# Gated cross-attention and mixture-of-experts block: the second expert product with the high and low part of its weights side by side

## The reference, cut to what matters

```python
x = x + tanh(g_xattn[0]) * xattn(layernorm(x), ctx_768, Wq, Wk, Wv, Wo, bo)
# feed-forward: top 2 of 8 experts, capacity cap = 2 * (4096 / 8) = 1024
de = disp.reshape(E, cap, Dm)                                  # 8 x 1024 x 256
h = relu(einsum('ecd,ehd->ech', de, fc1_w) + fc1_b)            # hidden width 1024
eo = einsum('ech,ehd->ecd', h, fc2_w) + fc2_b                  # back to width 256
out = sum(gathered * (gates * w)[:, :, None], axis=1)
x = x + tanh(g_ffn[0]) * out
```

## Time and profile before

| | |
|---|---|
| median of 3 runs | 991.46 us (989.94 to 992.4) |
| the profiled execution | 994.87 us |
| its span, first to last instruction | 993.1 us |
| mean granted TensorE clock | 0.983 |
| TensorE matmul / weight load busy | 949.4 us (96%) / 823.4 us (83%) |
| VectorE, ScalarE, GpSimd busy | 676.3 us (68%), 508.1 us (51%), 281.8 us (28%) |

### The profile page before, as it was taken

The page is one execution under the profiler, slowest core; times in us unless marked ns, Lnnn a source line. Parts: engine busy times, 40 slices in busy tenths (PEclk is TensorE's granted clock), DMA queues, the critical chain, the costliest instruction groups (busy, mean ns, idle before and its releaser), DMA issues.

```text
span 993.1 us, 18998 instructions
## 1 busy us (share of the span) xinstructions
PE 949.4 (96%) x7199; PEld 823.4 (83%) x7199; DVE 676.3 (68%) x1542; ACT 508.1 (51%) x1573; POOL 281.8 (28%) x293
## 2 busy tenths in 40 slices
PE   7799999999999999999999888999999999999996
PEld 5587877888878878878888786999999999999995
DVE  5768687686785886886776862757575665657572
ACT  3567376465664773673754621535444343435352
POOL 6803025024033043042041133222222223232222
PEclk8989999999999999999999998999999999999998
DMA  9096003011020021021011015254342435252521
GB/s 259 22 298 194 22 2 107 23 41 67 22 86 24 22 92 38 2 86 44 1 44 44 13 52 187 66 117 101 76 128 50 128 49 130 49 130 56 141 53 22
DMA packets 63099, 76.63 MB, mean 77 GB/s; under 512 B 6033, under 2 KB 55096, under 8 KB 63008
## 3 DMA queue, kind: packets, MB, share of 16 engines
q1 hardware_dynamic: 50720, 59.18, 20.0%
q0 software_dynamic: 12288, 16.23, 9.0%
HBM read 46.52 MB, written 29.49 MB: 77 GB/s over the span
## 4 chain that ended last, share of the span: by engine, by line
PE 73%; ACT 11%; DVE 8%; POOL 3%; DMA 2%; issue 2%; SPq 1%; POOLq 0%; DVEq 0%; another core or an unknown queue 0%
PE down L1211 6%; PE down L1210 6%; PE down L1209 6%; PE up L1195 6%; PE up L1196 6%; PE up L1197 6%; PE score L545 4%; ACT probs_odd L733 4%; ACT work L733 4%; PE out_bank L533 4%; PE probT L520 4%; DVE negmax L913 2%; PE rT L1179 2%; PE query_bank L466 2%; PE query_bank L464 2%
## 5 line engine op out<-in xcount | busy, mean ns | idle before, releaser
L1151 POOL DMA_INDIRECT out_dram<-eo,index x64 | 99.4, 1553 | 282.2 <-ACT eo L1253 250.4
L1245 ACT ACTIVATE hid<-up,b 128x512 f32<-128x512 f32 x128 | 88.3, 690 | 84.8 <-PE up L1197 84.8
L733 ACT ACTIVATE probs_odd<-score,negmax 128x128 f32<-128x128 f32 x256 | 91.3, 382 | 44.6 <-DVE negmax L913 44.6
L733 ACT ACTIVATE work<-score,negmax 128x128 f32<-128x128 f32 x256 | 91.4, 383 | 42.8 <-DVE negmax L913 42.8
L407 POOL DMA_INDIRECT disp<-packed,slots x64 | 68.8, 1075 | 133.8 <-DVE slots L904 92.4
L913 DVE TENSOR_REDUCE negmax<-score 128x4 f32<-128x512 f32 x128 | 82.0, 682 | 28.1 <-PE score L545 27.7
L698 ACT ACTIVATE k_sb<-key_bank 128x512 f32<-128x512 f32 x64 | 38.8, 606 | 112.8 <-PE key_bank L489 111.5
L1253 ACT ACTIVATE eo<-eo_raw,gate 128x256 f32<-128x256 f32 x64 | 30.9, 506 | 122.4 <-DVE eo_raw L1315 122.4
L1306 DVE TENSOR_TENSOR hid_l<-hid,hid_h 128x512 fp32r<-128x512 f32 x128 | 88.6, 693 | 4.4
L921 DVE COPY pT<-probT 128x512 f32<-128x512 f32 x128 | 82.2, 682 | 8.7 <-PE probT L520 7.4
L1315 DVE TENSOR_TENSOR eo_raw<-down,b 128x256 f32<-128x256 f32 x64 | 25.8, 423 | 86.4 <-PE down L1211 86.4
(11 more groups left out here) (253 smaller groups left out, 2788.8 us busy)
## 6 DMA issues: line engine op xcount, KB each, us to landing
rows<-disp SPq DMA_DIRECT2D x18, 516.0 KB, 5.4
w_raw<-fc1T_dram SPq DMA_DIRECT2D x9, 1024.0 KB, 8.3
w_raw<-fc_dram SPq DMA_DIRECT2D x9, 1024.0 KB, 10.9
disp<-fixed SPq DMA_DIRECT2D x1, 8256.0 KB, 33.8
rows<-x_dram SPq DMA_DIRECT2D x16, 512.0 KB, 4.3
out_dram<-rows SPq DMA_DIRECT2D x8, 512.0 KB, 3.1
c_raw<-ctxT_dram SPq DMA_DIRECT2D x8, 256.0 KB
c_raw<-ctxT_dram SPq DMA_DIRECT2D x16, 128.0 KB
```

The costliest lines, as they stand in the source:

```text
L733: last = nc.scalar.activation(probs[w % 2][:, c, :], score[hh][:, b * P:(b + 1) * P], ACT.Exp, bias=negmax[:, w % 2, c:c + 1], accum_out=s ...
L1151: pool.indirect_dma_start(out=out_rows[:, :], out_offset=bass.IndirectOffsetOnAxis(ap=index[half][:, i:i + 1], axis=0), in_=eo[half][:, i, ...
L1245: nc.scalar.activation(hid[m % 2][:, :], up[m % 2][:, :], ACT.Relu, bias=b1[par][:, m:m + 1]).then_inc(s_hid, 1)
```

## The change

The two halves of the split second weights become one tensor, with high and low part of the same `k` next to each other. One matmul of 512 columns multiplies `hid_h` with both; its result for the low part lands in the upper 256 columns of the bank. The product `hid_l` x high part stays a matmul of 256 columns and adds into the lower half. For the last `k` the small matmul goes first, so that the wide one is the last of its block. VectorE then adds the bias to the upper half into a new tile `small_part`, waits for that instruction by a semaphore, and adds the lower half. `wo_h` and `wo_l` of the attention become views of the new tensor. ScalarE and VectorE write the weight parts through the same views, with the same element counts.

```diff
-        w2_split = [... sbuf_tensor(f"w2_split{n}", [P, HK, D], mybir.dt.float32r)) for n in range(2)]
+        w2_both = keep.enter_context(nc.sbuf_tensor("w2_both", [P, HK, 2, D], mybir.dt.float32r))
...
-    (wq_h, wq_l), (wo_h, wo_l) = w1_split, w2_split
+    wq_h, wq_l = w1_split
+    wo_h, wo_l = w2_both[:, :, 0, :], w2_both[:, :, 1, :]
...
-    w2_h, w2_l = [w2_split[0], sb("w2_h1", [P, HK, D], f32r)], [w2_split[1], sb("w2_l1", [P, HK, D], f32r)]
+    w2 = [w2_both, sb("w2_both1", [P, HK, 2, D], f32r)]
...
+    small_part = sb("small_part", [P, GB, D])
...
                 t = slice(i * P, (i + 1) * P)
-                o = down[i][:, 0:D]
-                mm(o, hid_h[:, k, t], w2_h[par][:, k, :], start=(k == 0), stop=False)
-                mm(o, hid_h[:, k, t], w2_l[par][:, k, :], start=False, stop=False)
-                last = mm(o, hid_l[:, k, t], w2_h[par][:, k, :], start=False, stop=(k == HK - 1))
+                if k == HK - 1:
+                    mm(down[i][:, 0:D], hid_l[:, k, t], w2[par][:, k, 0, :], start=False, stop=False)
+                last = mm(down[i][:, :], hid_h[:, k, t], w2[par][:, k, :, :].rearrange("p s d -> p (s d)"), start=(k == 0),
+                          stop=(k == HK - 1))
+                if k < HK - 1:
+                    mm(down[i][:, 0:D], hid_l[:, k, t], w2[par][:, k, 0, :], start=False, stop=False)
                 if k == HK - 1:
                     last.then_inc(s_down_ready, 1)
...
-            nc.scalar.activation(w2_h[par][:, :, :], w2_raw[:, :, :], ACT.Copy).then_inc(s_w_hi, 1)
+            nc.scalar.activation(w2[par][:, :, 0, :], w2_raw[:, :, :], ACT.Copy).then_inc(s_w_hi, 1)
...
-            V.tensor_tensor(w2_l[par][:, :, :], w2_raw[:, :, :], w2_h[par][:, :, :].bitcast(f32),
+            V.tensor_tensor(w2[par][:, :, 1, :], w2_raw[:, :, :], w2[par][:, :, 0, :].bitcast(f32),
                             ALU.subtract).then_inc(s_w_lo, 1)
...
-                V.tensor_tensor(eo_raw[:, i, :], down[i][:, 0:D], b2[par][:, :], ALU.add).then_inc(s_eo_raw, 1)
+                V.tensor_tensor(small_part[:, i, :], down[i][:, D:2 * D], b2[par][:, :], ALU.add).then_inc(s_small_part, 1)
+                dve.wait_ge(s_small_part, 4 * n + i + 1)
+                V.tensor_tensor(eo_raw[:, i, :], down[i][:, 0:D], small_part[:, i, :], ALU.add).then_inc(s_eo_raw, 1)
```

More of the change, by code:

```diff
@@ L96, in gated_block @@
         w1_split = [keep.enter_context(nc.sbuf_tensor(f"w1_split{n}", [P, DK, H], mybir.dt.float32r)) for n in range(2)]
-        w2_split = [keep.enter_context(nc.sbuf_tensor(f"w2_split{n}", [P, HK, D], mybir.dt.float32r)) for n in range(2)]
+        w2_both = keep.enter_context(nc.sbuf_tensor("w2_both", [P, HK, 2, D], mybir.dt.float32r))
         s_e0_lo = sem("e0_lo")
-        shared = (s_e0_lo, first, blank, running, tanh_g, ident, w1_raw, w2_raw, w1_split, w2_split)
+        shared = (s_e0_lo, first, blank, running, tanh_g, ident, w1_raw, w2_raw, w1_split, w2_both)
         block = keep.enter_context(nc.Block())
@@ L126, in sb @@
         return ctx.enter_context(nc.sbuf_tensor(name, shape, dt))
-    s_e0_lo, first, blank, running, tanh_g, ident, w1_raw, w2_raw, w1_split, w2_split = shared
-    (wq_h, wq_l), (wo_h, wo_l) = w1_split, w2_split
+    s_e0_lo, first, blank, running, tanh_g, ident, w1_raw, w2_raw, w1_split, w2_both = shared
+    wq_h, wq_l = w1_split
+    wo_h, wo_l = w2_both[:, :, 0, :], w2_both[:, :, 1, :]
     wk_h, wk_l, wk_d = (sb(n, [P, INNER], f32r) for n in ("wk_h", "wk_l", "wk_d"))
@@ L1084, in experts @@
         s_rt_ready, s_rt_hi, s_rt_split, s_up_ready, s_hid, s_hid_hi, s_hid_split, s_down_ready, s_eo_raw,
-        s_eo_raw2, s_eo_ready, s_scatter0, s_scatter1, s_meta, s_dve_self, s_pool_gate,
+        s_eo_raw2, s_small_part, s_eo_ready, s_scatter0, s_scatter1, s_meta, s_dve_self, s_pool_gate,
     ) = (sem("e_" + name) for name in (
@@ L1088, in experts @@
         "rt_ready", "rt_hi", "rt_split", "up_ready", "hid", "hid_hi", "hid_split", "down_ready", "eo_raw",
-        "eo_raw2", "eo_ready", "scatter0", "scatter1", "meta", "dve_self", "pool_gate",
+        "eo_raw2", "small_part", "eo_ready", "scatter0", "scatter1", "meta", "dve_self", "pool_gate",
     ))
```

## The result

The changed kernel takes 991.99 us (median of 22 runs, 990.25 to 993.6), the kernel before 990.09 us (22 runs, 988.43 to 992.4). The ratio is 1.0018, 95% interval 1.0011 to 1.0025: **slower by 0.18% or 1.8 us** (the medians differ by 1.9), with little doubt about the sign, where 3.5 us less was forecast. The forecast of 987.9 us counted from 991.46 for the kernel before, which took 1.4 less this time; so the change is further off the forecast (5.4) than the time itself (4.1).

The account below looks back on a forecast made before the run. TensorE's own gapless stream was taken as the bound in the expert part. 11 long down products saving 0.35 us each (3.84) less 0.29 lost at the end gave -3.55: 991.46 - 3.55 = 987.9 us, range 985.0 to 992.0.

Parts of the forecast that it names:

- A set in the long products: Down products of 11.39 us: the matmuls per `k` and block fall from 353.1 to 342.2 ns, saving 0.35 us a product.
- The short products: The 4 of 16 down products at 10.98 us: matmuls per `k` and block stay at 340.0 ns, no gain.
- It is not the place of the data: Down products: the extra 4.4 ns per narrow matmul is not from data place; groups 3 and 4 read the same weights.
- The second addition: VectorE, each block: sums come 0.46 us later, costing 0 at the 15 boundaries between groups of the expert part.
- The end, +0.29: Last group through the final scatter: 0.46 us delay less 0.17 us gain from 16 sets of matmuls, so +0.29 us.
- The layout costs nothing: Weight splits keep their element counts; the output projection reads the same numbers at other addresses: 0.
- rival 1: Down products: only columns count, so merging gains nothing and the tail costs 0.46 us: 991.9 us; 22%.
- Rival 4: Down products all turn to 353.1 ns per `k` and block; with tail and projections +3.4 us, 994.8 us; 8%.
- rival 2: Down products: extra time stays on every matmul, 348.8 ns per `k` and block; 1.5 saved, 0.39 lost, 990.3 us; 12%.
- rival 3: Down products: narrow matmul, freed from the weight load ahead, streams at the clock; 333.4 ns a set, 983.8 us; 8%.
- rival 5: All down products: small fixed part per matmul, 2.2 ns; 512 sets save 1.1 us, tail takes 0.46: 990.8 us; 5%.
- The 3.41 us between the profiled execution and the median: Whole kernel: median lies 3.41 us below the profiled execution, taken as speaking for mostly short down products without a profiler.

Follow-up runs that it names:

- the repeat of before: The kernel before run again with no edit, against the kernel before: ratio 0.9999 (0.9989 to 1.0009).

## Why the prediction was wrong, point by point

- *TensorE's stream is the bound.* Right: no idle time after either.
- *A set in the long products costs 342.2, between 340.0 and 344.4.* **This is the step that failed.** It measured 353. The wide step was taken from the up product, whose stationary operand is `w1_h`; with `hid_h` in that role a wide matmul steps at 233 to 235, shown by exchanging the one operand (3.72 against 3.82 us for 16) and by moving `hid_h` alone by 64 bytes. That row was also one of wide matmuls in a run: even with `hid_h` at its better place the sequence of the change takes 346 to 353 a set, not 342.2. Even the upper bound of a set, 348.8, was too low, since it gave the wide matmul 4.4 ns more and it has over 8. What in the chip makes the place count stays open.
- *The short products stay at 340.0 a set.* Also wrong: they went to 353, four times 0.38 us. I had counted their pace as safe; it is one of two paces taken on entry, and the new sequence never takes it. With the long ones 0.04 shorter each, this is the whole +1.1 us.
- *"It is not the place of the data",* argued from groups 3 and 4 reading the same weights. The conclusion went too far: at a fixed place there are two narrow paces, as the projection shows too, but the place of the stationary operand sets which there are.
- *The second addition comes 0.46 us later and costs nothing at the 15 boundaries.* Right: 0.46 measured, no wait of TensorE; in the kernel before it costs only the end.
- *The end, +0.29.* The mechanism is right, the size too small by the gain that did not come. The last scatter starts 14.16 us after the last down product (966.82 to 980.98), where it was 13.72 and 14.0 was expected: +0.44.
- *The layout costs nothing.* Right, ratio 1.0002.
- *The time, by luck.* 991.99 us is within 0.1 of rival 1's 991.9. But rival 1 has the kernel 0.46 us slower than before, and 1.8 was measured; it counted from 991.46, and this time the kernel before took 990.09. By the same luck 991.99 lies inside the range, at its very end, while the direction was wrong.
- *Rival 1.* One of its two reasons, a wide matmul of 235.4 ns, is what the long products show. The prediction spoke against it because wide matmuls fall to 226.7, which it had read with the other stationary operand. What rival 1 left out is that the short products turn long.
- *Rival 4* names what happened in time (all products at 353 a set: +1.7, the end +0.46, together +2.1 without the projections; 1.8 measured). Its cause is right in one half, the wide matmul is slow per column, and wrong in the other: it put that down to how a product is entered, and moving `hid_h` alone changed the wide step. Its term for the projections (1.2 us) has nothing to do with the change, as the repeat of before shows.
- *Rivals 2, 3 and 5* fell: each has a set under 351 ns in the long products, and it takes 353. The figure of the Trainium skill behind rival 5 is N / 2.4 GHz plus 2.5 ns ("TensorE: Matmul & The Clock Gate", section "Wait — 56ns, not 53.3ns?"). It holds for none of the settled float32r steps here: 226.7 to 241 ns stand against 215.8, and 113.3 to 120 against 109.2.
- *The 3.41 us between the profiled execution and the median* were no sign of short products: the repeat has 5 instead of 4. They lie in the attention, whose length scatters by several us (4.0 between the trace before and that of its repeat).

## What to carry to other kernels

Where TensorE streams without a gap, as in this expert part, merging matmuls at the same number of columns gains only what the step per column improves; take that step from a row with the same operands in the same roles, in the same order, not from one with the same shape. An extra instruction on the engine that empties the banks was free in the middle of the run, where 0.47 us of waiting covered its 0.46, and was paid in full at the end. With differences near 0.2%, compare the traces stretch by stretch and not by their spans: here the spans had the wrong sign.

## What the runs showed of the hardware

- The place of the **stationary** operand sets the step of the matmul: wide 226.7, 233 or 228 to 241 ns, narrow 120, 117.7 or 113.3, or 112 to 124 in turn, at 0, 64 and 128 spare bytes. 1088 bytes behave as 64, so what counts repeats after 1024 bytes or sooner. Whether it is the place by itself or against that of the moving operand was not separated. Removing 64 bytes from the kernel before makes it slower by 0.47%. A wide step of 235 ns has room for the next load: in the trace after it starts 4 ns behind the matmul (694.117) and takes 187. The Trainium skill says that loading the next weights takes no read bandwidth from the running matmul (same page, section "Step-by-step: what each phase is for"). Here the place of what is loaded changes the step, so the two are not independent; whether bandwidth is what is lost was not tried. At a narrow matmul the load takes longer than the step (188 ns against 113.3 in the trace before), and every matmul of every run has a load of its own; so whether the loads set the narrow steps was not tried either.
- At 64 bytes narrow matmuls have two paces, 113.3 and 117.7 ns, and one that is taken in the first few steps is kept for 90 and more. In the projections the same code goes at either from one execution to the next. The pace goes with a few ns at the entry (in all 96 down products of the six traces with the narrow matmuls and 64 bytes, a second step of 120 to 122 stands before 113, one of 117 to 119 before 118), and not with the order of the operands; whether those ns are its cause was not tried. Why the fast one follows wide matmuls with `hid_h` in most runs of narrow ones at that place, and the slow one those with `w1_h`, stays open.
- Behind narrow matmuls, wide ones of the up product take about five steps (233, 236, 228, 233, 231 ns) to reach 226.7. A sequence that alternates the two does not settle there: 228 to 231 in the best blocks and 235 to 236 in the last one, with `hid_h` without spare bytes and `hid_l` 64 off.
